# Where a group's first key pair is transposed: end of the fifth unit's jobs, or head of the sixth's

## The reference, cut to what matters

```
q = rms_norm(x @ wq, q_norm_w);  k = rms_norm(x @ wk, k_norm_w);  v = x @ wv
k_ctx = rms_norm(h_ctx_kv @ wk_ctx, k_norm_w);  v_ctx = h_ctx_kv @ wv_ctx
q, k = rope(q), rope(k)
scores = einsum(q, concat(k_ctx, k)) * scale + mask     # 16 heads share 4 key heads
out = softmax(scores) @ concat(v_ctx, v) @ wo
```

## Time and profile before

| | us |
|---|---|
| median of 3 runs | 1284.8 (1284.22 to 1286.25) |
| profiled execution, its own time | 1283.05 |
| its span | 1281.2 |
| PE busy | 1174.8 (92%) |
| DVE busy | 1030.4 (80%) |
| ACT busy | 823.5 (64%) |
| POOL busy | 805.6 (63%) |

### The profile page before, as it was taken

How to read it: one execution, slowest core, us unless ns; L and a number is a source line. 1 busy time by engine, 2 the same in 40 slices (tenths; PEclk the granted TensorE clock), 3 DMA queues, 4 the chain that set the end, 5 groups by cost and what they waited for, 6 DMA issues and landing times.

```text
span 1281.2 us, 30330 instructions
## 1 busy us (share of the span) xinstructions
PE 1174.8 (92%) x11419; PEld 878.0 (69%) x11419; DVE 1030.4 (80%) x1979; ACT 823.5 (64%) x1917; POOL 805.6 (63%) x1010
## 2 busy tenths in 40 slices
PE   4998699999999999999999999999999986678898
PEld 2544377777778777777778777777777765455557
DVE  6876778888888888889888888889888897786673
ACT  4765567767777777766767676776767544446431
POOL 2765386967768696867768695867869443851000
PEclk9998899999999999999999999999999998889999
DMA  8630179778997877798697779878787978000000
GB/s 290 203 95 4 31 141 178 151 150 159 189 170 157 164 157 159 145 180 187 146 170 149 165 151 164 153 147 163 151 166 153 195 181 207 1 1 1 1 1 34
DMA packets 542689, 173.32 MB, mean 135 GB/s; under 512 B 520368, under 2 KB 535232, under 8 KB 542288
## 3 DMA queue, kind: packets, MB, share of 16 engines
q1 hardware_dynamic: 541520, 167.96, 63.0%
q0 software_dynamic: 1024, 3.42, 1.1%
HBM read 33.05 MB, written 8.26 MB: 32 GB/s over the span
## 4 chain that ended last, share of the span: by engine, by line
PE 73%; DVE 15%; DMA 3%; POOL 3%; ACT 3%; issue 3%; SPq 0%; POOLq 0%; DVEq 0%; ACTq 0%
PE PS L1254 15%; PE PS L1256 14%; PE PS L1255 14%; PE PS L1401 8%; PE PS L1397 7%; PE PS L1398 7%; DVE mx L1766 5%; DVE pl L1786 3%; DMA pT_l<-pl 2%; PE PS L1350 2%; PE PS L733 1%; PE PS L711 1%; DMA blk<-in_c_blk 1%; PE PS L1359 1%; DVE f_s L1693 1%
## 5 line engine op out<-in xcount | busy, mean ns | idle before, releaser
L1766 DVE TENSOR_REDUCE mx<-PS 128x1 f32<-128x512 f32 (+2 forms) x512 | 296.1, 621 | 112.4 <-PE PS L1256 110.8
L1397 PE MATMUL PS<-v_h,pT_h 128*128 128x129 f16 (+1 forms) x1856 | 224.9, 221 | 4.9 <-DMA pT_h<-ph 4.8
L1398 PE MATMUL PS<-v_l,pT_h 128*128 128x128 f16 (+1 forms) x1856 | 224.8, 220 | 0.0
L2003 POOL CAST ph<-pr_end 128x705 f16<-128x705 f32 (+1 forms) x128 | 111.0, 867 | 171.6 <-ACT pr_end L1557 171.5
L1557 ACT ACTIVATE pr<-PS,nb 128x1024 f32<-128x1024 f32 x128 | 144.3, 1128 | 69.4 <-DVE nb L1774 69.4
L1254 PE MATMUL PS<-kT_h,qT_h 128*128 128x512 f16 (+2 forms) x512 | 181.9, 355 | 7.7 <-ACT pr L1557 7.7
L1397 PEld LDWEIGHTS PS<-v_h,pT_h 128*128 128x128 f16 (+1 forms) x1856 | 182.4, 98 | 8.4 <-DMA pT_h<-ph 5.5
L1398 PEld LDWEIGHTS PS<-v_l,pT_h 128*128 128x128 f16 (+1 forms) x1856 | 182.4, 98 | 2.7
L1255 PE MATMUL PS<-kT_l,qT_h 128*128 128x512 f16 (+2 forms) x512 | 181.0, 353 | 0.0
L1256 PE MATMUL PS<-kT_h,qT_l 128*128 128x512 f16 (+2 forms) x512 | 180.9, 353 | 0.0
L1786 DVE TENSOR_TENSOR pl<-pr,ph 128x1024 f16<-128x1024 f32 x128 | 175.8, 1373 | 0.0
(11 more groups left out here) (285 smaller groups left out, 2911.5 us busy)
## 6 DMA issues: line engine op xcount, KB each, us to landing
stage<-in_ctxT SPq DMA_DIRECT2D x8, 800.5 KB, 6.7
weights_kept<-relay SPq DMA_DIRECT2D x30, 128.0 KB, 2.2
relay<-in_w_lanes SPq DMA_DIRECT2D x14, 204.9 KB, 3.5
stage<-in_wq SPq DMA_DIRECT2D x4, 512.0 KB, 3.9
stage<-in_wo SPq DMA_DIRECT2D x4, 512.0 KB, 3.9
pT_h<-ph SPq DMA_TRANSPOSE x128, 4.1
pT_l<-pl SPq DMA_TRANSPOSE x128, 3.6
ctx_kept<-ctx_h SPq DMA_DIRECT2D x2, 800.5 KB, 8.4
```

What stands on the lines that cost most here:

```text
L1397: mm(PS[:, OB, 0:DH + 1], pT_h[0:rows, slot, t, :], v_h[0:rows, par, v, :], start=t == 0, stop=False)
L1398: mm(PS[:, OB, 0:DH], pT_h[0:rows, slot, t, :], v_l[0:rows, par, v, :], start=False, stop=False)
L1766: dve.reduce_max(mx[:, c:c + 1], PS[:, c, 0:cols(u % LT, c)], AX_X).then_inc(mx_part, 1)
L2003: pool.tensor_copy(ph[:, slot, HALF:LAST + w], pr_end[:, 0:BANK + w]).then_inc(pool_hi, 1)
```

## The change

kq1 leaves the end of unit 4's list and becomes the first job of unit 5. The sequence of all jobs stays the same, and so do the banks that each takes.

```diff
            [("piece", 7), ("piece", 8)],
-           [("kq", 5), ("piece", 9), ("kq", 4), ("q", 1), ("kq", 1)],
-           [("kq", 2), ("kq", 3)],
+           [("kq", 5), ("piece", 9), ("kq", 4), ("q", 1)],
+           [("kq", 1), ("kq", 2), ("kq", 3)],
            [("out", 2), ("out", 3)],
```

## The result

| | us |
|---|---|
| before, median of 6 runs | 1285.27 (1284.22 to 1287.17) |
| changed, median of 6 runs | 1280.95 (1278.29 to 1282.47) |
| ratio, 95% interval | 0.9958 (0.9945 to 0.9971) |
| profiled execution, its own time | 1279.19 |
| its span | 1277.4 |

The changed kernel is faster by 4.3 us in the medians. The profiled executions differ by 3.9 us (1283.05 and 1279.19). The forecast was 3.6.

What follows compares the result with a forecast made beforehand. PE's queue was taken to bound the attention; typically 0.69 us won before unit 7's scores less 0.45 given back, 3.6 us over 15 groups, takes 1284.8 to 1281.2 us, range 1277.5 to 1285.2.

Steps and rivals of the forecast that it cites:

- What bounds the kernel: In the attention PE's own queue sets the time; its recurring stop is kq1's wait for L1762, 14.1 us over 16 times.
- The stall is worth 1.01 us: End of unit 4: without kq1, `pv` of unit 4 starts 1.50 us earlier, 0.49 being kq1's work and 1.01 the stall.
- The exponential becomes the later release: Before unit 7's scores: PE waits 0.81 us for ACT's exponential of unit 6, so they start only 0.69 earlier.
- kq2 behind the scores gives 0.45 back: After unit 7's scores: two steps stand instead of one, costing 0.45 us and leaving `pv` of unit 5 0.24 earlier.
- The sum, 3.6 us: Gains over all 15 groups: 2.7 us from eleven, 0.4 from three, 0.5 from group 6.
- DVE at its limit in unit 6: Unit 6: DVE's 0.21 us wait for PE is used up, but DVE does not set the pace.
- A: The whole stall at kq1 is won and PE never meets the exponential: 13.2 us, 1271.6; chance 0.06.
- B: ACT's exponential of unit 6 comes no earlier without kq1's copy: 5.0 us slower, 1289.8; chance 0.07.
- C: ACT's smaller gain, late low-part landings at `pv` of unit 4, or DVE spend 1 to 3 us: 1282.5 to 1284.8; chance 0.21.

Runs made afterwards that it cites:

- x1: The changed kernel with ACT's f16 weight copy (relay) moved from the end of unit 4 to the end of unit 5; 1274.81 us, ratio 0.9902 to before.
- x2: The kernel before with ACT's weight copy (relay) moved from unit 4 to unit 5; 1285.39 us, ratio 1.0006.
- d1: The kernel before with ACT's weight copy done twice, the second after the first has ended; 1296.15 us, ratio 1.0081.
- d2: The changed kernel with ACT's weight copy done twice, the second after the first has ended; 1291.23 us, ratio 1.0043 to before.
- x3: The changed kernel with PE alone doing kq1 and kq2 ahead of the scores of unit 7; 1277.08 us, ratio 0.9927 to before.
- e0_after: The changed kernel run again, unaltered, beside the kernel before; 1279.45 us, ratio 0.9950.
- p1: PE follows the changed job lists, ACT and DVE keep those of the kernel before; 1316.86 us, ratio 1.0253 to before.

## Why the prediction was right

1. *What bounds the kernel.* Right: PE was the queue that counts, and the one recurring wait was the place. The wait for L1762 is gone from the groups.
2. *The stall is worth 1.01 us and the place before `pv` of unit 4 moves by 1.50.* Measured 1.57 in group 12, 707.58 - 703.92 = 3.66 against 5.20 in group 9, so 1.54. A single transpose of 65 columns costs PE 0.06 and not the 0.11 that I took from the wide ones.
3. *The exponential becomes the later release; the scores of unit 7 are 0.69 earlier.* Measured 0.70 in group 9 (711.27 - 703.92 = 7.35 against 8.05). The pieces of this term came out too: ACT's step of 0.57 (2.85 to 2.28), the 0.06 from ACT's end to PE. x1, x2, d1 and d2 show that this release sets the time of the stage in the changed kernel, and stands just ahead of PE in the kernel before.
4. *kq2 behind the scores gives 0.45 back.* From the scores of unit 7 to `pv` of unit 5 there are 3.32 us, as forecast (2.87 before). x3 shows that the term is real, since putting kq2 ahead again wins it.
5. *The sum, 3.6 us.* The 15 groups give 3.5 in the traces. The medians give 4.3, and the interval of the ratio goes from 3.7 to 7.1 us, so that the forecast lies just below it. In e0_after the ratio was 0.9950 (0.9925 to 0.9975), which holds it. The 0.7 us beyond 3.6 aren't explained by this place. PE's waits for transposed exponentials over the attention sum to 7.6 us before, 8.9 in the changed kernel and 6.6 in its second trace, so they alone differ by 2.3 between two executions of one kernel. That the median came out within 0.3 us of the 1281.2 forecast is in part luck: three more runs moved the median of before from 1284.8 to 1285.27, and the larger gain made up for it.
6. *DVE at its limit in unit 6.* Right: the idle time of 0.21 ahead of the maxima is gone, and `rden` lies 0.05 earlier against `rden` of unit 3 (15.24 instead of 15.29; forecast 0.03), while PE is 0.25 ahead:

```profile
717.24 1.40 DVE L1760 SCALAR_TENSOR_TENSOR kT_l<-PS,wcol,kT_h 128x512 f16<-128x512 f32 x2
718.56 0.68 DVE L1796 SCALAR_TENSOR_TENSOR relay<-relay 128x512 f16<-128x512 f32 x1
719.16 0.16 DVE L1801 RECIPROCAL rden<-PS 128x1 f32<-128x1 f32 x1
719.32 1.34 DVE L1766 TENSOR_REDUCE mx<-PS 128x1 f32<-128x512 f32 x2
```

Of the rivals, A (13 us) is ruled out by the new wait. B (the exponential stays) did not happen, and p1 shows what its mechanism is worth: if the copy for kq1 does hold the exponential back, the change loses instead of winning. C needs late landings; they occurred in two of 15 groups and were covered by the wait. The gap's length, 12.5 us in this stretch, was not the gain, 3.5. The Trainium skill, "Perfetto Trace Analysis", section "Optimization Strategy", says to find the gaps on the engine that one optimizes for, and what blocks it there. The trace agrees as to the place.

## What to carry to other kernels

The length of a stall is not what its removal wins; look for the release that comes next, on every other engine, and subtract. (Where the pause also lowers the clock, as below, it can cost more than its length.) Here three stood close behind one another: ACT's exponential 0.2 us behind DVE's remainder, POOL's normalisations half a microsecond behind ACT's. Each edit paid only up to the next one. The cheap test is a pair: make the same small edit to the second release with and without the first in place. Here it was worth nothing in one and 0.45 of its 0.52 us in the other.

When jobs share a ring of buffers, moving one changes who waits for whom three places on; before a job is moved, read off for each engine what stands between it and the emptying of its buffer.

## What the runs showed of the hardware that I had not expected

A pause of PE can cost more than its length. With 2.30 us of idle time in each of 15 groups (p1_pe_order_alone), the granted clock was at the lower level behind 7 of them, for 3.4 us each, and the scores' steps went from 0.22 to 0.43 us. Behind the pauses of 0.68 us (the changed kernel, 13 groups) and of 1.35 us (d2_after_delay, 13 groups) it was never lowered.
